# A two-layer attention kernel on one core: layer 1's instruction order rewritten, the first batch's MLP placed among the second's top-16 halves, the second's end in a three-tile and a one-tile part

## What is computed

```python
# layer 0 (a DiT block)
x = x + gate_a * (softmax(q k^T / sqrt(8)) v @ W_proj + b)        # 512 x 512 per head
x = x + (softmax(q_c k_c^T / sqrt(8)) v_c @ W_cproj + b)          # against 77 context tokens
x = x + gate_m * (gelu(mod(ln(x)) @ W_mlp1 + b) @ W_mlp2 + b)     # 128 -> 512 -> 128
# layer 1
x = x + g_msa * (window_attention(mod(ln(x))) @ w_so + b)         # windows of 64, rolled by 32
s = q k^T / sqrt(8)                                               # against 77 context tokens
top_s, top_i = top_k(s, 16)
x = x + g_mca * (softmax(top_s) v[top_i] @ w_co + b)
a, b2 = split(mod(ln(x)) @ w_m1 + b_m1)                           # 128 -> 2 x 512
x = x + g_mlp * ((silu(a) * b2) @ w_m2 + b)                       # 512 -> 128
```

## Time and profile before

| | |
|---|---|
| median of 3 runs | 459.71 us (458.87 to 459.73) |
| profiled execution, its own time | 461.02 us |
| its span, first to last instruction | 459.3 us |
| around the span | 1.7 us |
| mean granted TensorE clock | 0.859 |
| busy: TensorE, VectorE, ScalarE, GpSimd | 366.4, 303.5, 204.1, 109.4 us |
| layer 0's attention, up to its last product with the values | 0 to 162 us |
| layer 0's cross attention | 161 to 221 us |
| layer 0's MLPs | 221 to 244 us |
| layer 1's window attention, up to the first MAX8 | 244 to 314.4 us |
| layer 1's top-16 halves, up to the end of D15 | 314.4 to 417.4 us |
| the rest | 417.4 to 459.3 us |

### The profile page before, as it was taken

How to read it: one execution, slowest core, us unless ns; L and a number is a source line. 1 busy time by engine, 2 the same in 40 slices (tenths; PEclk the granted TensorE clock), 3 DMA queues, 4 the chain that set the end, 5 groups by cost and what they waited for, 6 DMA issues and landing times.

```text
span 459.3 us, 8983 instructions
## 1 busy us (share of the span) xinstructions
PE 366.4 (80%) x3326; PEld 214.9 (47%) x3326; DVE 303.5 (66%) x1281; ACT 204.1 (44%) x304; POOL 109.4 (24%) x130
## 2 busy tenths in 40 slices
PE   0958899999989987899979798866585566675885
PEld 0746322323333155677646547643363344453454
DVE  4386976999897056667236544236979999995332
ACT  1141036666656935566532032433444455654411
POOL 8047200002510011001022400011443544443010
PEclk9977658999999998999989586977877777776989
DMA  7236031112000000000000000000000000000000
GB/s 211 59 112 185 24 123 53 52 55 87 3 1 2 0 1 1 1 2 1 1 0 2 6 2 6 4 3 1 1 3 0 1 2 1 1 1 1 1 24 24
DMA packets 10811, 12.16 MB, mean 26 GB/s; under 512 B 2378, under 2 KB 9103, under 8 KB 10767
## 3 DMA queue, kind: packets, MB, share of 16 engines
q1 hardware_dynamic: 10469, 11.55, 8.6%
q0 software_dynamic: 256, 0.01, 0.0%
q10 hardware_dynamic: 42, 0.01, 0.0%
HBM read 8.69 MB, written 2.62 MB: 25 GB/s over the span
## 4 chain that ended last, share of the span: by engine, by line
PE 55%; DVE 28%; ACT 8%; issue 5%; POOL 1%; DMA 1%; SPq 1%; ACTq 0%; DVEq 0%
PE psum L1350 6%; PE psum L1410 6%; PE psum L1378 5%; PE psum L1363 5%; DVE mx L1125 4%; DVE left L1180 4%; DVE left L1187 4%; PE psum L1511 4%; PE psum L1251 3%; PE psum L1393 3%; DVE top L1177 3%; PE psum L1421 3%; DVE top L1184 2%; PE psum L1433 2%; PE psum L1448 2%
## 5 line engine op out<-in xcount | busy, mean ns | idle before, releaser
L1125 DVE TENSOR_REDUCE mx<-psum 128x1 f32<-128x512 f32 x128 | 80.2, 680 | 11.2 <-PE psum L1350 11.1
L731 ACT ACTIVATE big<-psum 128x1024 f32<-128x1024 f32 x64 | 62.4, 1022 | 42.3 <-PE psum L1363 42.0
L1350 PE MATMUL psum<-KS,QS 72*128 72x512 bf16 x128 | 51.1, 431 | 5.3 <-DVE mx L1125 4.4
L1410 PE MATMUL psum<-kblk,qf 128*128 128x308 f32 x128 | 48.0, 508 | 1.1 <-DVE qf L1058 0.8
L1421 PE MATMUL psum<-ident,pr 128*77 128x128 f32 x256 | 39.3, 305 | 9.9 <-POOL pr L672 9.8
L561 POOL TENSOR_TENSOR rstd<-vareps,minus_half 128x4 f32<-128x4 f32 x12 | 12.2, 1018 | 143.5 <-DVE vareps L901 143.4
L1421 PEld LDWEIGHTS psum<-ident,pr 128*77 128x77 f32 x256 | 35.3, 171 | 18.1 <-POOL pr L672 13.3
L1363 PE MATMUL psum<-QS,KS 75*128 75x512 bf16 x128 | 40.4, 404 | 0.4
L672 POOL TENSOR_TENSOR pr<-pr,early 128x616 f32<-128x616 f32 x16 | 23.9, 1493 | 56.0 <-ACT early L841 38.8
L1378 PE MATMUL psum<-big,V 128*9 128x512 f32 x256 | 35.2, 623 | 0.5 <-ACT big L731 0.5
L1350 PEld LDWEIGHTS psum<-KS,QS 72*128 72x128 bf16 x128 | 12.0, 103 | 47.4 <-DVE mx L1125 24.6
(11 more groups left out here) (195 smaller groups left out, 663.3 us busy)
## 6 DMA issues: line engine op xcount, KB each, us to landing
QS<-scr_q SPq DMA_DIRECT2D x8, 288.0 KB
KS<-scr_k SPq DMA_DIRECT2D x8, 288.0 KB
scr_q<-qp SPq DMA_DIRECT2D x2, 384.0 KB, 2.7
scr_k<-kp SPq DMA_DIRECT2D x2, 384.0 KB, 3.3
early<-in_L_xcond_w_ada_dram SPq DMA_DIRECT2D x1, 576.0 KB, 7.2
wmlp<-in_L_xcond_W_mlp_dram SPq DMA_DIRECT2D x2, 256.0 KB, 3.2
scr_k<-kp SPq DMA_DIRECT2D x2, 256.0 KB, 3.5
wm<-in_L_xcond_w_m_dram SPq DMA_DIRECT2D x1, 512.0 KB, 4.4
```

The source lines that it names most:

```text
L731: freed(act.activation(pT[:, u % 2, 1024 * half:1024 * (half + 1)], ps, ACT.Exp), "sT", 0, u, half)
L1125: freed(dve.tensor_reduce(mx[:, n % 3, NT * hh + q:NT * hh + q + 1], ps, AX_X, ALU.max), "max", t, q)
L1350: filled(pe.matmul(ps, QS[b][0:ROWS, h, q * P:(q + 1) * P], KS[b][0:ROWS, h, :], start=True, stop=True), "max", j, q)
L1410: last = pe.matmul(ps[:, 512 * a:512 * a + HH // 2 * S], qf[:, b, i * P:(i + 1) * P], kb[:, c0:c0 + HH // 2 * S], start=True, stop=True)
```

## The change

1. Layer 1 is driven by one string `ORDER` that all engines walk through (`layer1`). A letter is a piece of work, the digits its half, unit, or (layer norm or projection, batch, part). An item with "<" is done there by TensorE alone, the same item with ">" there by the other engines, and one without a sign by all.
2. In the windows the first batch's chain (o200, p300, s400, n400, t400, q0) stands earlier: o200 follows G3 at once, before E5.
3. The first batch's MLP (m000 to m003, then r00) stands among the halves 10 to 15. Its silu is worked out without the Silu function: ACT takes tanh(x/2) and x/2 in two ACTIVATEs, POOL multiplies and adds in two TENSOR_TENSORs (`swish`), and VectorE's `gate_mul` waits for them.
4. The second batch's last cross attention, layer norm and MLP are split in parts 1 (tiles 0 to 2) and 2 (tile 3), after `TILES`. Part 1's transposes (o311) stand before D15. ACT starts one of the last transfers.
5. In both layers the scores use `kown` instead of `kblk`: an array of 32 rows, one quarter of the heads, for each of the two matmuls (rows r = 0 and 1, or 2 and 3). POOL builds it once for both layers with half the elements of one `kblk`, and `ctx_blocks(1)` is gone. The buffer `left` is no longer shared with layer 1's spread weights, and `mask4` and `half_b` are two small VectorE instructions at the start.
6. The scores of layer 1 have only the room W0; W1 is for the MLP's pairs (`mlp_in_pair`).

The diff, cut to its core:

```diff
+ORDER = """
+    a00 a01 a02 a03 n310 v0 x000 x001 x010 x011 x020 x021 x030 x031 y0 t310 a10 a11 a12 a13 v1
+    x100 x101 x110 x111 x120 x121 x130 x131 y1
+    E00 E01 E10 E11 F0 E20 E21 F1 G0 E30 E31 F2 G1 E40 E41 F3 G2 G3 o200 E50 E51 p300 s400 S400 F4 G4 E60 E61 n400 N400
+    F5 G5 t400 E70 E71 q0 Q0
+    Q1 A0 B0 d0 C0 D0 F6
+    K0 Q2 G6< A1 B1 G6> d1 T0 F7 C1 D1
+    K1 Q3 G7< A2 B2 G7> d2 T1 o210 C2 D2 V0<
+    K2 V0> Q4 U0< p310< A3 B3 U0> p310> s410 d3 S410 T2 C3 D3 n410
+    K3 Q5 t410 A4 B4 d4 N410 T3 q1 C4 D4 V1<
+    K4 V1> Q6 U1< A5 B5 U1> d5 T4 C5 D5
+    K5 Q7 A6 B6 d6 T5 C6 D6 V2<
+    K6 V2> Q8 U2< A7 B7 U2> d7 T6 C7 D7
+    K7 Q9 A8 B8 d8 T7 C8 D8 V3<
+    K8 V3> Q10 U3< A9 B9 U3> d9 T8 o300 C9 D9
+    K9 Q11 p400< A10 B10 p400> s500 d10 S500 T9 C10 D10 n500 V4<
+    K10 V4> Q12 U4< t500 A11 B11 U4> d11 N500 T10 m000< C11 D11
+    K11 Q13 A12 B12 m000> d12 T11 m001< C12 D12 V5<
+    K12 V5> Q14 U5< A13 m001> B13 U5> d13 T12 m002< C13 D13
+    K13 Q15 A14 m002> B14 d14 T13 m003< C14 D14 V6<
+    K14 V6> U6< A15 m003> B15 U6> d15 T14 o311 r00< C15 D15 r00>
+    K15 p411 s511 S511 T15 n511 N511 t511 V7 m110 U7 m111 o312 m112 p412 s512 S512 m113 n512 r11 N512 t512
+    m120 m121 m122 m123 r12
+    """
+
+
+TILES = [(0, NT), (0, NT - 1), (NT - 1, 1)]
...
+def layer1(side):
+
+    for item in ORDER.split():
+        if item[-1] == ("<" if side == ">" else ">"):
+            continue
+        digits = item[1:].rstrip("<>")
+        if item[0] in "ABCDQKTVUd":
+            yield item[0], (int(digits),)
+        else:
+            yield item[0], tuple(int(c) for c in digits)
...
-        kblk = sb("kblk", [P, B, H, S])
+        kown = sb("kown", [P, 2, B, G, S])
...
+            store(sp, 0, 0)
+            store(sp, 1, 1)
+            store(sp, 1, 2, first=True)
+            sp.wait_ge(s_out, 16 * OUT_DMAS)
...
+            def own_keys():
+
+                pool.wait_ge(s_mask4, 1)
+                for l2 in range(2):
+                    wait_read(pool, "kc", l2)
+                    pool.tensor_tensor(kown[:, l2, :, :, :], kcT[:, l2, :, :].unsqueeze(2).broadcast_to([P, B, G, S]),
+                                       mask4[:, :].unsqueeze(1).unsqueeze(3).broadcast_to([P, B, G, S]), ALU.mult)\
+                        .then_inc(s_kown, 1)
...
+            def swish(b, c):
+
+                pool.wait_ge(s_half, c + 1)
+                pool.tensor_tensor(sa[b][c % 2], sa[b][c % 2], gT[:, b, c, :], ALU.mult).then_inc(s_swish, 1)
+                pool.wait_ge(s_swish, 2 * c + 1)
+                pool.tensor_tensor(gT[:, b, c, :], sa[b][c % 2], gT[:, b, c, :], ALU.add).then_inc(s_swish, 1)
...
+            def silu_out(b, p, c):
+
+                i0, ni = TILES[p]
+                own = slice(i0 * P, (i0 + ni) * P)
+                ps = read_room(act, "m", b, p, c)[:, own]
+                v = VECS["L1_b_m1"] + c
+                if b == 0:
+                    if c >= 2:
+                        act.wait_ge(s_swish, 2 * (c - 1))
+                    act.activation(sa[0][c % 2], ps, ACT.Tanh, scale=0.5, bias=half_b[:, c:c + 1])
+                    act.activation(gT[:, 0, c, :], ps, ACT.Identity, scale=0.5, bias=half_b[:, c:c + 1])\
+                        .then_inc(s_half, 1)
+                else:
+                    if c >= 2:
+                        wait_read(act, "m", b, p, c - 2)
+                    act.activation(sa[b][c % 2][:, own], ps, ACT.Silu, bias=cols[:, v:v + 1]).then_inc(s_silu, 1)
...
+            def gate_mul(b, p, c):
+
+                i0, ni = TILES[p]
+                own = slice(i0 * P, (i0 + ni) * P)
                 v = VECS["L1_b_m1"] + NC_ + c
-                ps = read_room(dve, "mlpb", b, c)
-                wait_read(dve, "mlp", 1, b, c)
-                freed(dve.scalar_tensor_tensor(out=gT[:, b, c, :], in0=ps[:, 0:N], scalar=cols[:, v:v + 1],
-                                               in1=sa[b][c % 2], op0=ALU.add, op1=ALU.mult), "mlpb", b, c)
-
...
+                ps = read_room(dve, "m", b, p, c)[:, N + i0 * P:N + (i0 + ni) * P]
+                if b == 0:
+                    dve.wait_ge(s_swish, 2 * (c + 1))
+                    swished = gT[:, 0, c, :]
...
+                    swished = sa[b][c % 2][:, own]
+                freed(dve.scalar_tensor_tensor(out=gT[:, b, c, own], in0=ps, scalar=cols[:, v:v + 1],
+                                               in1=swished, op0=ALU.add, op1=ALU.mult), "m", b, p, c)
...
-                    pe.wait_ge(s_kblk, B * layer + b + 1)
-                kb = kblk[:, b, :, :].rearrange("p h s -> p (h s)")
+                    pe.wait_ge(s_kown, layer + 1)
+                kb = kown[:, layer, b, :, :].rearrange("p k s -> p (k s)")
                 ps = open_room(pe, "sc", layer, e)
                 for a in range(2):
-                    c0 = S * (HH * (e % 2) + HH // 2 * a)
-                    last = pe.matmul(ps[:, 512 * a:512 * a + HH // 2 * S], qf[:, b, i * P:(i + 1) * P],
-                                     kb[:, c0:c0 + HH // 2 * S], start=True, stop=True)
+                    r = 2 * (e % 2) + a
+                    rows = slice(QUAD * r, QUAD * (r + 1))
+                    last = pe.matmul(ps[:, 512 * a:512 * a + G * S], qf[rows, b, i * P:(i + 1) * P], kb[rows, :],
+                                     start=True, stop=True)
```

1312 lines of the change are left out of this document (672 added, 640 removed).

## The result

The changed kernel takes 478.72 us (median of 4 runs, 474.34 to 480.58), the kernel before 459.29 us beside it. The ratio is 1.0416, 95% interval [1.0364, 1.0469]: 19.4 us slower.

What follows compares the result with a forecast made beforehand. Bounds: VectorE's queue in layer 1's halves, TensorE with ScalarE behind it in layer 0's cross attention, one long chain at the end. Terms -3.8 - 3.5 + 19.0 - 12.9 = -1.2 us, from 459.71 to 458.5 us; range 452 to 464.5.

Steps and rivals of the forecast that it cites:

- Step (a): Scores from 32-row arrays, gain expected in layer 0's cross attention: -3.8 us, bounds 0 and -8.3.
- Eight tiles give 3.4 us: Layer 0's cross attention: one of a tile's two scores gives its 0.42 us back, over eight tiles.
- rival 4: 32-row scores don't overlap or array switches eat the gain: their term is 0 or above, time 462; chance 0.14.
- one score that ran at the low clock 0.4 more: Part of the 32-row scores' gain: 0.4 us more from one score that ran at the low clock.
- rival 3: Slower by TensorE's low clock in the end: if 7 us are added, the time is 465; chance 0.18.
- Step (b): First batch's chain moved up in the windows: first MAX8 3.5 us earlier, bounds -1 and -5.5.
- Step (c): Layer 1's halves: added VectorE work +4.6, projection wait -1.9, gate_mul's waits +16.3; +19.0 us in all.
- The wait of 2.3 for the projection goes: Layer 1's halves: VectorE's projection wait vanishes, the query may wait 0.4 longer: -1.9 us.
- ScalarE's order is what makes it: Halves 12 to 15: gate_mul's 16.3 us of waits come from the MLP's two ACTIVATEs queued late on ScalarE.
- Step (d): The end, from D15, with the split second batch: 29.0 us against 41.9, so -12.9 us; bounds 26 and 36.
- R: End of r00, put 2.8 us behind D15 (2.2 at full clock, 6 at half); the span's end at R + 24.7.

Runs made afterwards that it cites:

- swish_moves: dve_swish with VectorE's division, the second batch's residual and its query read later in the halves: 450.64 us, ratio 0.9824 to the kernel before.
- dve_swish: Changed kernel with 128-row scores in both layers, tanh and identity earlier, and a chunk's two GpSimd operations replaced by one on VectorE: 457.43 us, ratio 0.9992.
- b_twice: Kernel before with layer 0's scores from 32 rows, each pair issued twice: 475.26 us.
- before_own_l0: Kernel before with 32-row scores in layer 0 alone: 466.50 us.
- early_swish: Changed kernel with tanh, identity and the two GpSimd operations of each MLP chunk moved earlier, gate_mul behind B in four halves: 471.61 us.
- before_own: Kernel before with 32-row scores in both layers and nothing else changed: 468.68 us, ratio 1.0231.

## Why the prediction was wrong

**Step (a) failed, in two ways.** "Eight tiles give 3.4 us" took a score at 0.62 us, where it takes 0.72, and was worked out as if the rest of a tile stayed as it was. At full clock both scores together save 0.64 us a tile, the work around them takes 0.48 more, and 0.17 us is left for the 0.42 of the forecast. The larger part of the 0.48 is the mechanism of rival 4: four switches of 0.08 us each, half of the 0.15 that the rows allowed. The rest is ScalarE's queue, which the prediction had named, and which took its share beside the switches. The larger error is that the clock was taken as given: "one score that ran at the low clock 0.4 more" reads the low clock as something that passes. The stretch from layer 0's cross attention to the first keys of layer 1 took +6.2 us instead of -3.8, because 32-row scores bring the clock down for some 25 us there. I had looked for a clock risk as a rival of its own (rival 3) in the end only, where TensorE has gaps. Here the fall starts behind one gap of 1.31 us (up to 188.72), of which the kernel before has the like (1.15), and then lasts through 25 us without any.

The trace of before may have had a sign of it. Over the windows, whose scores come from 32-row arrays, it has

```profile
245.90:314.40 68.50, 56.15 (x1317) 39.67 (x1316) 29.37 (x62) 19.91 (x35) 10.23 (x7) 0.76 0.01 4
```

a granted clock of 0.76 with TensorE busy for 82% of the time, where layer 0's cross attention has 1.00 with 89%. I used that stage for the speed of 32-row products and not for its clock. That it is low for the same reason was not tried.

**Step (b) was right as a sum, and by luck in part.** -3.4 measured, -3.5 forecast. The stage's clock is 0.76 as before, so the gain is most likely the order's; no run tried it alone. The parts are off and cancel. The first batch's residual is read at 307.28, less the 6.2 of the stage before at 301.1, so it comes 0.6 us earlier than before (301.72) and not 1.8: o200 starts early enough (302.57, less 6.2 is 296.4, for the 297.3 forecast), but the projection behind it takes 2.08 us, at the low clock, for 1.06. From the residual to the first MAX8 it is 317.20 - 307.28 = 9.9 us against 314.43 - 301.72 = 12.7 before, a gain of 2.8 where 2.8 - 1.1 = 1.7 was forecast.

**Step (c) had the right mechanism and was 4.9 us short.** The added work is right: without waits the halves take 127.0 - 22.65 = 104.3 us against 103.05 - 3.26 = 99.8, +4.5 for a forecast 4.6. gate_mul's waits are 19.0 for 16.3; the 2.7 is half 13, where the sum had ScalarE's copies back to back, which was wrong, since MLP chunk, V5 and Q14 stand in one queue on TensorE and the chunk was at the low clock. "The wait of 2.3 for the projection goes" was wrong by the other 2.3: the projection's wait fell to 1.03, but the query's grew from 0.41 to 1.97, and two divisions wait 0.34 each where two scores had waited 0.27. The stall moved on to the next read. My reason for the 16.3, "ScalarE's order is what makes it", was a third of it: reordering ScalarE and GpSimd took 6.4 of 18.8 us, taking GpSimd's two operations away took the other 12.4.

**Step (d) was 3.0 us short.** r00's end came 5.5 us behind D15 and not 2.8, since r00 ran at the low clock (6.62 us). The prediction had R at "6 at half" and "2.2 at full clock", and chose 2.8, nearly the full clock. From there to the end it is 476.1 - 449.65 = 26.5 us, for 24.7 + 1.5 = 26.2 forecast.

The four errors (measured less forecast) are 10.0, 0.1, 4.9 and 3.0 us, 18.0 in sum, which is the difference between a span 16.8 us longer and the forecast -1.2. All have the same sign, and beside a bound in (b) the range had treated the low clock as a case of its own of 7 us in one place. It took part in all four steps.

## What to carry to other kernels

Two 32-row matmuls side by side were shorter than two of 128 rows here (0.72 us for 1.04 at full clock), and took the clock away from all that stood around them: price such a change with the stage at both levels of the clock, and look at the granted clock of the stages that already work that way. A wait is not one engine's order: before moving an instruction out of it, follow the ring of queues once around, since the next queue takes its place. And when work was hidden here under an engine that is already full, what mattered was that nothing in that engine's queue waited for it; where the work lay was then worth nothing that shows.

## What the runs showed of the hardware

A 128x512 operation of VectorE with both inputs in SBUF ((tanh + 1) times half, in swish_moves) takes 0.67 us alone and 1.45 us where a GpSimd operation runs beside it:

```profile
393.87 1.24 POOL L731 TENSOR_TENSOR early<-gates,top 128x616 f32<-128x616 f32 x1
...
394.20 1.45 DVE L1191 SCALAR_TENSOR_TENSOR big<-qf,big 128x512 f32<-128x512 f32 x1
...
401.92 0.67 DVE L1191 SCALAR_TENSOR_TENSOR big<-xhat,big 128x512 f32<-128x512 f32 x1
```

The overlap is 395.11 - 394.20 = 0.91 us and the loss 0.78: VectorE got little done in it. In dve_swish the order was the other way around, VectorE's operation came first, and GpSimd's took 1.68 us instead of 1.22.

The low clock can stay while TensorE has no idle time at all: 24.92 us of work in 25.00 us in the changed kernel, and 12.00 in 12.00 in b_twice. And the same kernel can fall or escape, by time and mean clock: one execution in six escaped in before_own_l0, one in four in early_swish, none in the changed kernel and in before_own. What that hangs on stays open.
